# A language-conditioned adapter layer on one core: who copies the second W1 matrix of each pair into its slot

## The reference, cut to what matters

```python
h = einsum('bsh,bha->bsa', x, W1[ids]) + b1[ids]
h = relu(h)
y = x + einsum('bsa,bah->bsh', h, W2[ids]) + b2[ids]
mean, var = y.mean(-1), square(y - mean).mean(-1)
out = x + (y - mean) * rsqrt(var + 1e-5) * gamma[ids] + beta[ids]
```

## Time and profile before

| | us |
|---|---|
| median of 3 runs (lowest, highest) | 327.07 (326.28, 327.14) |
| the profiled execution | 328.89 |
| its span in the profile | 326.9 |

### The profile page before, as it was taken

How to read it: one execution, slowest core, us unless ns; L and a number is a source line. 1 busy time by engine, 2 the same in 40 slices (tenths; PEclk the granted TensorE clock), 3 DMA queues, 4 the chain that set the end, 5 groups by cost and what they waited for, 6 DMA issues and landing times. The chain is left out here.

```text
span 326.9 us, 7388 instructions
## 1 busy us (share of the span) xinstructions
PE 293.4 (90%) x2008; PEld 254.4 (78%) x2039; DVE 294.9 (90%) x621; ACT 235.6 (72%) x543; POOL 185.9 (57%) x217
## 2 busy tenths in 40 slices
PE   2757799999999999999999999999899799989972
PEld 1146678898998888889878878888788688879851
DVE  6998778999999999989998989799998789998986
ACT  3976367778888777778776777677767677768772
POOL 2952444666655556666565655566655636665552
PEclk9978599999999999999999999999999999999998
DMA  5999999999999999999999999999999999999954
GB/s 156 339 395 354 299 333 387 368 338 340 348 361 352 365 307 341 345 344 340 347 349 329 360 342 349 339 355 369 318 340 350 350 338 329 356 322 348 362 217 184
DMA packets 64792, 109.22 MB, mean 334 GB/s; under 512 B 4315, under 2 KB 15639, under 8 KB 64625
## 3 DMA queue, kind: packets, MB, share of 16 engines
q1 hardware_dynamic: 64654, 108.62, 96.6%
q10 hardware_dynamic: 99, 0.14, 0.1%
HBM read 44.78 MB, written 33.55 MB: 240 GB/s over the span
## 5 line engine op out<-in xcount | busy, mean ns | idle before, releaser
L346 POOL TENSOR_TENSOR x_io<-x_io,beta_all 128x512 f32<-128x512 f32 x128 | 162.4, 1280 | 46.2 <-DVE ps_y L617 39.4
L477 PE MATMUL ps_h<-x_T,w_stage 128*128 128x128 f32 x1024 | 128.5, 280 | 7.6 <-DMA w_stage<-w_all 7.5
L477 PEld LDWEIGHTS ps_h<-x_T,w_stage 128*128 128x128 f32 x1024 | 121.7, 195 | 11.9 <-DMA w_stage<-w_all 11.2
L409 ACT ACTIVATE cut<-ps_y,row_sum 128x512 bf16<-128x512 f32 x128 | 88.0, 687 | 32.0 <-PE ps_y L498 28.3
L636 DVE SCALAR_TENSOR_TENSOR ps_y<-ps_y,neg_mean,gamma_all 128x512 f32<-128x512 f32 x128 | 91.1, 753 | 10.6 <-ACT cut L409 9.5
L649 DVE SCALAR_TENSOR_TENSOR x_io<-ps_y,rstd,x_io 128x512 f32<-128x512 f32 x128 | 90.2, 747 | 2.5 <-DVE rstd L641 0.3
L463 PE MATMUL ps_T<-identity,x_io 128*128 128x128 f32 x512 | 69.0, 280 | 8.7 <-DMA x_io<-in_x 6.8
L463 PEld LDWEIGHTS ps_T<-identity,x_io 128*128 128x128 f32 x512 | 61.7, 144 | 18.0 <-issue 10.1
L498 PE MATMUL ps_y<-w_high,h_high 128*128 x128 | 62.4, 488 | 6.3 <-DVE w_low L598 4.0
L389 ACT COPY x_T<-ps_T 128x1024 f32<-128x1024 f32 x64 | 63.6, 993 | 2.9 <-PE ps_T L463 2.8
L617 DVE SCALAR_TENSOR_TENSOR ps_y<-x_io,b_all 128x512 f32<-128x512 f32 x93 | 63.0, 705 | 0.0
(11 more groups left out here) (66 smaller groups left out, 141.8 us busy)
## 6 DMA issues: line engine op xcount, KB each, us to landing
x_io<-in_x SPq DMA_DIRECT2D x64, 512.0 KB, 5.7
out<-x_io SPq DMA_DIRECT2D x63, 512.0 KB, 4.8
w_stage<-w_all SPq DMA_DIRECT2D x116, 256.0 KB, 3.5
w_stage<-in_L_cond_W SPq DMA_DIRECT2D x12, 256.0 KB, 6.2
x_io<-in_L_cond_W SPq DMA_DIRECT2D x5, 512.0 KB, 7.8
b_all<-in_L_cond_b SPq DMA_DIRECT2D x1, 2560.0 KB, 13.8
w_all<-in_L_cond_W SPq DMA_DIRECT2D x5, 512.0 KB, 7.7
out<-x_io SPq DMA_DIRECT2D x2, 256.0 KB, 2.0
```

Of the source, the lines that this page charges most:

```text
L346: nc.gpsimd.tensor_tensor(x_slot(t), x_slot(t), of_lang(beta_all, lang), ALU.add).then_inc(x_beta_ready, 1)
L409: nc.scalar.activation(squares[:, t % 2, :], ps_y[t % Y_BANKS][:, :], ACT.Square, scale=-float(H), bias=stat(row_sum, t), accum_out=stat(s ...
L477: last = nc.tensor.matmul(bank[:, b * S:(b + 1) * S], w1_stage[:, 2 * (p % STAGE_PAIRS) + b, c, :], x_T[:, (2 * p + b) % 4, c, :], start=F ...
```

## The change

From pair 6 on, the copy of the second batch's W1 is no longer a DMA. ScalarE does it, as `copy_w1(p + 3)`, placed in its step p between `copy_x(p + 1)` and `high_h(p)`. For that ScalarE loads two ids into registers in each of these steps, which it did not do before. SyncE issues one W1 DMA for each pair instead of two. TensorE's first products of a pair wait for one DMA's and one ScalarE copy's semaphore. Nothing else moves.

```diff
@@ SyncE, stage_w1 @@
-                for b in range(2):
+                for b in range(1 if scalar_copies(q) else 2):
                     sp.dma_start(w1_stage[:, 2 * (q % STAGE_PAIRS) + b, :, :], table[:, bass.ds(langs[b], 1), :, :])\
                         .then_inc(w1_staged[q % STAGE_PAIRS], 16)
@@ ScalarE @@
+            def copy_w1(q):
+
+                lang = langs_of(act, q)[1]
+                if q == STAGE_HBM:
+                    act.wait_ge(s_w1, 16 * W_CHUNKS)
+                act.wait_ge(h_summed, q - STAGE_PAIRS + 1)
+                nc.scalar.copy(w1_stage[:, 2 * (q % STAGE_PAIRS) + 1, :, :].rearrange("p c a -> p (c a)"),
+                               w1_all[:, bass.ds(lang, 1), :, :].rearrange("p o c a -> p (o c a)")).then_inc(w1_copied, 1)
+
             def step(p):
...
                 if p < PAIRS - 1:
                     copy_x(p + 1)
+                q = p + STAGE_PAIRS - 1
+                if q < PAIRS and scalar_copies(q):
+                    copy_w1(q)
                 high_h(p)
@@ TensorE, first_products @@
-                pe.wait_ge(w1_staged[p % STAGE_PAIRS], 32 * (p // STAGE_PAIRS + 1))
+                pe.wait_ge(w1_staged[p % STAGE_PAIRS], w1_stagings(p))
+                if scalar_copies(p):
+                    pe.wait_ge(w1_copied, w1_copies(p))
```

More of the change, by code:

```diff
@@ L115, in build @@
         w1_staged = [sem(f"w1_staged{i}") for i in range(STAGE_PAIRS)]
+        w1_copied = sem("w1_copied")
         s_w2 = [sem(f"s_w2_{n}") for n in range(W_CHUNKS)]
@@ L186, in vector_seeds, with scalar_copies, w1_copies, w1_stagings @@
             return t + 1 - scalar_seeds(t)
+        def scalar_copies(q):
+            return q >= STAGE_HBM
+        def w1_copies(q):
+            return len([r for r in range(q + 1) if scalar_copies(r)])
+        def w1_stagings(q):
+            return sum(16 if scalar_copies(r) else 32 for r in range(q % STAGE_PAIRS, q + 1, STAGE_PAIRS))
         def wait_seed(engine, t):
@@ L448, in _ @@
             high_w2(4)
+            act.wait_ge(ids_ready, 1)
             for p in range(FIRST, PAIRS):
```

## The result

The changed kernel takes 317.72 us (median of 4 runs, 316.19 to 320.02) against 326.97 us (median of 4, 326.28 to 327.14): ratio 0.9727, 95% interval 0.9659 to 0.9795. Run again beside the first experiments it was 318.06 us against 328.37 us, ratio 0.9704 (0.9618 to 0.979). One of the seven runs behind the 328.37 was in the slow state, which the ratio leaves out; the median of the other six is 327.78. Forecast was 316.6 us in 314 to 324 us, and faster. The profiled execution took 316.75 us with a span of 315.0.

A forecast was written before the change was run, and what follows sets the result against it. The prediction took late W1 DMAs, from full DMA engines and SyncE's slow queue, to hold the loop above TensorE's pace. Terms -11.2 + 0.7 = -10.5 us took 327.07 to 316.6 us; forecast range 314 to 318.5, 314 to 324 with rival A.

The forecast's parts named there:

- The loop's own pace: TensorE's loop: bias matmuls 4.16 and 4.40 us apart, 4.28 for a pair; forecast loop about 4.31.
- -11.2 us for W1's wait: TensorE's weight load in the loop: its 11.2 us of waits for W1's DMA would go.
- the 0.7 us charged to the path: Loop: allowance of 0.7 us for chains of occasional long ScalarE register loads, with VectorE near full.
- Two causes together: W1 late from full DMA engines (4.56 us for a pair) and SyncE's slow queue (4.59); the change touches both.
- The proportion rule for the bytes: DMA engines: time falls in proportion to bytes, 4.56 x 5/6 = 3.80 us for a pair.
- ScalarE's copy: ScalarE's loop: 58 new SBUF-to-SBUF copies at 0.57 us, 0.71 at most, beside TensorE; cost on the path 0.
- ScalarE's turn of 3.98: ScalarE's loop: 3.41 us for a pair becomes 3.98 with the copy, 0.30 under TensorE's 4.28.
- ScalarE's register load: ScalarE, behind the copy of x: mostly hidden by its 0.99 us, 0.1 us showing for each pair.
- A: Rival: transfers stay a partial bound and about half of W1's waits stay, 321.5 us (318.5 to 324); chance 0.13.
- B: Rival: SBUF copies cost the DMA engines nothing; loop stays 4.49, within 1 us of 327; 0.06, shared with small ScalarE slowdown.
- C: Rival: ScalarE becomes the bound, register load fully exposed, 4.81 us for a pair, 345 us; chance with a loss 0.11.
- What would show it: Signs in the loop: W1 wait under 2 us, DMA share near 0.9, ScalarE near 90% busy, its wait down 25 us.

The follow-up runs named there:

- the first experiments: Runs on one chip with the changed kernel repeated as control: 318.06 us, ratio 0.9704 to the kernel before.
- e4: Kernel before the change, both W1 DMAs kept on SyncE, but from pair 6 on the second carries a quarter of its bytes: 317.16 us (0.968).
- e2: Changed kernel plus an 8 KB DMA into a spare tile, issued by SyncE in each turn: 317.53 us (0.969).
- e1: Changed kernel, but ScalarE issues the second W1 DMA in place of its copy, so all bytes still move: 323.23 us (0.987).
- e10: Changed kernel, but ScalarE copies both W1 matrices and the second once more into an unread tile: 341.07 us (1.045).
- e11: Changed kernel with ScalarE's register load ahead of the squares instead of behind the copy of x: 317.39 us (0.973).
- e8: Changed kernel with ScalarE's W1 copy behind the high part of h instead of ahead of it: 319.12 us (0.975).
- k1_before: The kernel before the change, unaltered, run once more with a profile: 326.24 us, one run.
- e3: Kernel before the change, both W1 DMAs kept on SyncE, plus ScalarE's register load and copy into an unread tile: 326.19 us (0.997).

## Why the prediction was right, point by point

**The loop's own pace.** Right. 4.16 and 4.40 us apart held nearly to pair 62 (0.4 and 0.8 us lost in two profiles); the forecast of 4.31 was slightly too high.

**-11.2 us for W1's wait.** The mechanism was right and the wait is gone. The size came from one profile. A second profile of the kernel before has 5.1 us of this wait and 8.4 us lost in all; with 12.3 the two average 10.4, against 0.6 for the changed kernel. The difference, 9.8 us, agrees with the two measured gains, 9.25 and 9.7 us (317.72 against 326.97, 318.06 against 327.78). That the number came so close, 316.6 against 317.72, is in part luck: with the 5.1 us of the second profile the same sum would have said 322.7, still faster and still in the range, and misses of opposite sign cancelled. The wait was taken from the upper end; against that, the 0.7 us charged to the path was not paid, and the other losses of the loop (1.1 us in the first profile, 3.3 in the second) went as well, though the sum left them in. The 1.1 us left over is inside the scatter of the four runs (316.19 to 320.02) and needs no cause.

**Two causes together.** Right that both are there and that the change relieves both, wrong that they stand side by side. Relieving either one ends W1's lateness: the bytes in e4 and e2, the queue in e1. SyncE's turn of 4.59 us was taken as a price of its own; with the DMA engines not full the same issues take 4.0, and the changed queue 3.2 instead of the forecast 4.0. And 345 GB/s was taken as what the DMA engines can move, where e1 moved 373. The proportion rule for the bytes (3.80 us for a pair at 1.25 of 1.5 MB) fits the measured share: 3.80 / 4.28 = 0.89, measured 0.91 from 160 to 280 us.

**ScalarE's copy.** 0.62 us, between the ends 0.57 and 0.71 that had been taken from the nearest rows. What it costs is 0.52, from start to start. ScalarE's turn of 3.98 was over-sized, since it added shown durations, whose ends overlap the next instruction when nothing waits; e10 gives 3.67. So the spare time was 0.6 us, not 0.30. The Trainium skill ("ScalarE: Activation LUTs", section "Rules for kernel authors") gives its budget for an activation whose bias is a [128,1] pointer operand, a condition that the prediction left out. The 0.72 us that it makes of 512 elements, an estimate, agrees with the 0.71 us of the activation with a per-partition bias in the earlier trace rows and is above the measured 0.62 of this copy without one.

**ScalarE's register load.** The step was right that 0.99 us of cover hides most of it: 8.7 us in 22 places, 0.15 on average, against 0.1 forecast. The medians taken from other engines (0.8) were too low; it became 1.33 because the engines load together now. Against the register-load floor of about 600 ns that the prediction takes from the Trainium skill ("DMA: Bandwidth & Descriptors", section "Latency and other measured facts"), the least of the earlier trace rows are 472 to 534 ns: they lie below it, where the prediction says that they agree with it. The 0.7 us charged to the path was not paid: e11 removes the exposed part and gains nothing clear of noise.

**The rivals.** A (transfers stay a partial bound) fell: no wait for W1, share 0.91. B (bytes inside SBUF are free) fell by e4, and by the two queues of e1, where such a byte costs 95% of another. C (a slower ScalarE turn) is real as a mechanism, but it begins with the third copy (e10, +4.5% over before), not with one; and its trigger, a load exposed in full, does not cost what I wrote, because ScalarE's load by itself takes 0.5 us (e8).

**What would show it.** ScalarE's busy share in the loop is 0.90, as written. Its wait for the first products fell by 37.6 us, more than the 25 asked for.

## What to carry to other kernels

Where DMA engines are full and an engine has room, move a copy inside SBUF to that engine: here 256 KB less for each pair took a share of 1.00 to 0.91 (160 to 280 us) and gave back all of the wait. A DMA queue that issues too late may be slow only because the DMA engines are full; here fewer bytes or a second issuing queue each put W1 back in time, but fewer bytes gained more than twice as much (10.6 us in e4, 4.6 in e1). Price a queued instruction by the distance of starts in a place where it never waits, not by its shown duration; the difference (0.52 against 0.62, and the same for its neighbours) was the difference between no room and room for a second copy. And take a wait's size from more than one profiled execution before it becomes the largest term of a sum.

## What the runs showed of the hardware

The DMA engines moved 344 to 351 GB/s with SyncE's queue alone and 362 and 363 with a second queue, all at shares of 1.00 to 1.02 in the stretches 60 to 150 and 150 to 300 us (e1 against the kernel before, k1_before and e3). A copy inside SBUF took them 0.95 of the time for each byte of the mix with HBM (e1). A register load from SBUF takes 0.5 us on ScalarE and TensorE when no other engine makes one, and 1.1 to 1.5 when four make one within 0.4 us; SyncE's took 1.48 even alone. ScalarE's back-to-back copies start 0.1 us before the one ahead is shown to end.
